# Three dense samples instead of one, and the MLP's ring tile moved into the attention

## The reference

```python
# layer 0: deformable convolution (4 groups x 9 points = 36 samples a token) and an MLP
xp = x @ w_in + b_in
h = gelu(batch_norm(depthwise_conv3x3(x)))
offset = h @ w_off + b_off
mask = softmax((h @ w_msk + b_msk).reshape(N, H, W, GROUP, P), axis=-1)
samp = corner(y0, x0, (1-wy1)*(1-wx1)) + corner(y0, x0+1, (1-wy1)*wx1) \
     + corner(y0+1, x0, wy1*(1-wx1)) + corner(y0+1, x0+1, wy1*wx1)
y = einsum('nghwpc,nhwgp->nhwgc', samp, mask) @ w_out + b_out
x = x + gamma1 * layer_norm(y)
x = x + gamma2 * layer_norm(gelu(x @ w_fc1 + b_fc1) @ w_fc2 + b_fc2)
# layer 1: causal attention over an image's 3136 tokens, then 8 experts of which 2 count
t = t + attention(layer_norm(t))
t = t + experts_top2(layer_norm(t))
```

## Time and profile before

| what | us |
|---|---|
| median of 3 runs | 8872.07 (8864.89 to 8880.12) |
| the profiled execution's own time | 8881.66 |
| its span, first to last instruction | 8879.9 |
| PE busy (weight loads beside) | 5273.8 (3409.6) |
| DVE busy | 5563.6 |
| ACT busy | 2767.3 |
| POOL busy | 6554.4 |

### The profile page before, as it was taken

How to read it: one execution, slowest core, us unless ns; L and a number is a source line. 1 busy time by engine, 2 the same in 40 slices (tenths; PEclk the granted TensorE clock), 3 DMA queues, 4 the chain that set the end, 5 groups by cost and what they waited for, 6 DMA issues and landing times.

```text
span 8879.9 us, 85702 instructions
## 1 busy us (share of the span) xinstructions
PE 5273.8 (59%) x24752; PEld 3409.6 (38%) x24752; DVE 5563.6 (63%) x12091; ACT 2767.3 (31%) x6449; POOL 6554.4 (74%) x6898
## 2 busy tenths in 40 slices
PE   4456575555755576555665567654757556564567
PEld 2234353333533354333443344432434333342345
DVE  4666666666666666666576656765666666665554
ACT  2223232323323233322333233332323233332233
POOL 6777777777777777777777777777777777777771
PEclk7778787777877788777887788876878778776778
DMA  7333333232333323333333333333233333222220
GB/s 104 72 75 69 74 70 78 66 75 69 70 77 68 76 66 73 75 72 71 68 77 70 74 68 73 75 75 68 67 79 70 73 68 65 73 65 65 62 64 15
DMA packets 851881, 625.60 MB, mean 70 GB/s; under 512 B 551018, under 2 KB 734562, under 8 KB 851472
## 3 DMA queue, kind: packets, MB, share of 16 engines
q0 software_dynamic: 221200, 452.62, 21.0%
q1 hardware_dynamic: 629600, 167.72, 11.4%
q10 hardware_dynamic: 672, 0.24, 0.0%
HBM read 549.46 MB, written 70.57 MB: 70 GB/s over the span
## 4 chain that ended last, share of the span: by engine, by line
POOL 59%; issue 22%; PE 9%; DVE 5%; DMA 4%; SPq 1%; ACT 1%; POOLq 0%; DVEq 0%; another core or an unknown queue 0%; ACTq 0%
POOL ring L707 59%; DMA ring<-column_table,idx_r 3%; PE bank L1508 2%; PE bank L1544 2%; DVE y L1042 1%; PE bank L1517 1%; PE bank L1432 1%; PE bank L1684 1%; PE bank L1596 1%; PE bank L1661 1%; SPq L523 0%; DMA wts_r<-corner_weight 0%; SPq L493 0%; DVE ring L1032 0%; DMA tokens<-z 0%
## 5 line engine op out<-in xcount | busy, mean ns | idle before, releaser
L707 POOL DMA_INDIRECT ring<-column_table,idx_r x6860 | 6530.9, 952 | 2146.0 <-issue 2069.6
L1032 DVE TENSOR_TENSOR ring<-ring,bank 128x4608 f32<-128x4608 f32 x196 | 970.1, 4949 | 1017.7 <-POOLq L718 1016.6
L1042 DVE TENSOR_REDUCE y<-ring 128x128 f32<-128x4608 f32 x196 | 1571.1, 8016 | 16.8 <-remote 14.6
L1489 PE MATMUL bank<-ident,xn 112*128 112x112 f32 x224 | 54.9, 400 | 1722.5 <-DVE xn L968 1722.5
L1508 PE MATMUL bank<-kT,qT 128*112 128x448 f32 (+3 forms) x1792 | 824.7, 552 | 159.2 <-DVE arena L1144 152.2
L1544 PEld LDWEIGHTS bank<-v,pT 112*112 112x112 f32 x6496 | 817.7, 181 | 264.2 <-issue 186.1
L1544 PE MATMUL bank<-v,pT 112*112 112x128 f32 x6496 | 851.7, 278 | 57.1 <-DVE pT L1177 57.0
L1144 DVE TENSOR_SCALAR_CACHE_REDUCE arena<-bank 112x448 f32<-112x448 f32 x672 | 416.2, 623 | 524.6 <-PE bank L1508 495.4
L1517 PE MATMUL bank<-ident,arena 112*112 112x112 f32 x3248 | 495.6, 273 | 395.4 <-ACT arena L828 395.3
L1489 PEld LDWEIGHTS bank<-ident,xn 112*128 112x128 f32 x224 | 37.1, 217 | 1731.7 <-issue 1731.7
L1432 PE MATMUL bank<-xflat,stripes 116*128 116x448 f32 (+1 forms) x1120 | 586.9, 649 | 110.7 <-ACT xflat L790 110.6
(11 more groups left out here) (179 smaller groups left out, 7291.8 us busy)
## 6 DMA issues: line engine op xcount, KB each, us to landing
ring<-column_table,idx_r POOLq DMA_INDIRECT x6860
xflat<-dense_rows SPq DMA_DIRECT2D x56, 406.0 KB
column_table<-proj SPq DMA_DIRECT2D x196, 112.0 KB
corner_weight<-wts_s SPq DMA_DIRECT2D x56, 252.0 KB
wts_r<-corner_weight SPq DMA_DIRECT2D x196, 72.0 KB
hT<-dense_rows SPq DMA_DIRECT2D x224, 56.0 KB
tin<-tokens SPq DMA_DIRECT2D x56, 224.0 KB, 3.1
out<-xn SPq DMA_DIRECT2D x56, 224.0 KB
```

Source lines behind the costliest of these rows:

```text
L707: pool.indirect_dma_start(ring[:, r, e * CORNERS:(e + 1) * CORNERS, :].rearrange("p s c -> p (s c)"), None, source, bass.IndirectOffsetOnA ...
L1032: dve.tensor_tensor(corners, corners, wts_p.unsqueeze(2).broadcast_to([128, GP * CORNERS, CG]), ALU.mult)\
L1042: dve.tensor_reduce(y[:, k % BLK % 2].rearrange("p (g c) -> p g c", g=G), ring[:, bass.ds(t % RING, 1)].rearrange("p o (g e) c -> p (o g) ...
```

## The change

It computes samples 33, 34 and 35 on PE (`DENSE = 3`) and gathers 33 (`FETCHED = GP - DENSE`). The rows stored and loaded, the places, the hats and the sums are there three times: 15 stages in a chunk (`STAGES`). Three stages (`EARLY`) stand ahead of the attention, so DVE's `set_places` moves ahead of the layer norm and xn is turned in bank 5; the other twelve stand in the row blocks, three to each. `keep_part` of the first sample stands in row block 0, of the second in row block 2, of the third in the front. The ring holds 33 samples, and `sum_up` reduces it in two instructions, of three whole groups and of the last one's six samples. `between` is gone from the MLP: h=0 now has tiles 0 (first), 1 (second), 2 (`extra`: multiplied behind q=2, reduced behind q=3) and 3 (third), h=1 has 4, 5 and 6. The memset of the ring's unused part is gone.

```diff
-FETCHED = GP - 1
+DENSE = 3
+FETCHED = GP - DENSE
+XN_BANK = 5
+EARLY = 3
+STAGES = DENSE * (NB // 2)
...
-        ring = sb("ring", [128, RING, GP * CORNERS, CG])
+        ring = sb("ring", [128, RING, FETCHED * CORNERS, CG])
...
+        rows = (xflat[0:2 * PAD], rows_b[:, :, :], rows_c)
+        place = (hT[0:2 * PAD, 1], rows_b[:, 0], rows_c[:, 0])
+        row_wts = (hT[:, 0], wts_b[:, :], wts_c[:, :])
...
-                        first, second, third, between = (
-                            ((p, n, 1), (p, n, 2), (p, n, 3), (p, n, 4)),
-                            ((p, n, 5), None, (p, n, 6), (p, n, BLK)))[h]
+                        first, second, extra, third = (
+                            ((p, n, 0), (p, n, 1), (p, n, 2), (p, n, 3)),
+                            ((p, n, 4), (p, n, 5), None, (p, n, 6)))[h]
...
-                sp.wait_ge(d_kept, FIRST + gd)
+                sp.wait_ge(d_kept, FIRST + DENSE * gd)
...
+                for k in range(DENSE):
+                    sp.dma_start(rows[k].rearrange("p a n -> p (a n)"),
+                                 row_d[gd, k, 0:2].rearrange("a n -> (a n)").partition_broadcast(2 * PAD))\
                         .then_inc(d_rows_in, 16)
+                    for dy in range(DY):
+                        sp.dma_start(row_wts[k][dy * CG:(dy + 1) * CG], row_d[gd, k, 2 + dy].partition_broadcast(CG))\
+                            .then_inc(d_rows_in, 16)
...
+                sample, pair = stage // (NB // 2), stage % (NB // 2)
+                if pair == 0:
+                    act.wait_ge(d_placed, FIRST + DENSE * gd + sample + 1)
...
+                if now:
+                    for stage in range(EARLY):
+                        hats(gd, stage)
                 act.wait_ge(xn_turned, FIRST + g + 1)
...
-                        hats(gd, q)
+                        hats(gd, EARLY + 3 * q)
...
                             exponentials(c + 2)
+                        if now and c == j // 3:
+                            hats(gd, EARLY + 3 * q + 1)
+                        if now and c == 2 * j // 3:
+                            hats(gd, EARLY + 3 * q + 2)
                     if q == 1 and second:
                         tile(*second)
-                if now:
-                    hats(gd, NT)
+                    if q == 3 and extra:
+                        tile(*extra)
...
+                step.did(dve.tensor_reduce(
+                    y[:, k % BLK % 2, 0:(G - 1) * CG].rearrange("p (g c) -> p g c", g=G - 1),
+                    products[:, 0:whole].rearrange("p (g e) c -> p g c e", g=G - 1), AX.X, ALU.add))
                 dve.tensor_reduce(
+                    y[:, k % BLK % 2, (G - 1) * CG:], products[:, whole:].rearrange("p e c -> p c e"), AX.X, ALU.add)\
                     .then_inc(y_made, 1)
...
-                if between:
-                    tile(*between)
...
+                else:
+                    dve.wait_ge(d_kept, FIRST + DENSE * gd + sample)
+                    step.did(dve.tensor_tensor(row_wts[sample], bank[0][:, 0:CH], row_wts[sample], ALU.mult))
+                    step.wait()
+                    dve.tensor_tensor(part[:, f % 2], part[:, f % 2], row_wts[sample], ALU.add).then_inc(d_kept, 1)
...
                     multiply(*first)
+                if now:
+                    set_places(dense_chunk(*now)[2])
                 dve.wait_ge(tok_in[buf], (s + h) * 16)
...
                 layer_norm(tin[:, buf], xn, NT, TT, 1e-5).then_inc(xn_made, 1)
-                if now:
-                    set_places(dense_chunk(*now)[2])
...
                             chunk_max(q + 1, c)
+                        if now and q == 0 and c == j // 3:
+                            keep_part(*now, 0)
+                        if now and q == 2 and c == 0:
+                            keep_part(*now, 1)
...
+                    if extra and q == 2:
+                        multiply(*extra)
+                    if extra and q == 3:
+                        sum_up(*extra)
...
-                        keep_part(*now)
+                        keep_part(*now, 2)
...
-                step.did(dve.memset(ring[:, :, FETCHED * CORNERS:, :], 0.0))
...
+                elif pair == 0:
+                    pe.wait_ge(d_kept, FIRST + DENSE * gd + sample)
...
                 banks_left(fronts, s * 2 + h, g)
+                if now:
+                    for stage in range(EARLY):
+                        sum_columns(di, gd, stage)
                 pe.wait_ge(xn_made, FIRST + g + 1)
...
-                        sum_columns(di, gd, q)
+                        sum_columns(di, gd, EARLY + 3 * q)
...
                         ins.then_inc(pv_made, 1)
+                        if now and c == j // 3:
+                            sum_columns(di, gd, EARLY + 3 * q + 1)
+                        if now and c == 2 * j // 3:
+                            sum_columns(di, gd, EARLY + 3 * q + 2)
...
-                if now:
-                    sum_columns(di, gd, NT)
```

More of the change, by code:

```diff
@@ L451, in slots @@
                             tile(p, n, k1 - 1)
-                        mlp(s, n, h, last, (p, fronts[h] + 1), g + 1 if att else 0, between, then)
+                        mlp(s, n, h, last, (p, fronts[h] + 1), g + 1 if att else 0, then)
             first_image()
@@ L621, in tile, with attention @@
                 ring_load(p, t)
-            def attention(i, j, h, s, fronts, first, second, now):
+            def attention(i, j, h, s, fronts, first, second, extra, now):
                 if first:
@@ L627, in attention, with mlp @@
                     tile(*second)
-            def mlp(s, n, half, last, fronts, n_att, between, then):
+                if extra:
+                    tile(*extra)
+            def mlp(s, n, half, last, fronts, n_att, then):
                 k0, k1 = PARTS[half]
@@ L793, in dense, with attention @@
             def dense(now):
[L794 removed]
+                for stage in range(STAGES):
                     hats(dense_chunk(*now)[2], stage)
[L797 removed]
+            def attention(i, j, h, s, fronts, first, second, extra, now):
                 g = i * NJ + j
                 gd = dense_chunk(*now)[2] if now else 0
+                if now:
+                    for stage in range(EARLY):
+                        hats(gd, stage)
                 act.wait_ge(xn_turned, FIRST + g + 1)
[L801 removed]
+                act.activation(xnT[:, :], bank[XN_BANK][:, 0:CH], ACT.Copy).then_inc(xnT_kept, 1)
                 act.wait_ge(qkv_made, FIRST + g * 3 + 1)
@@ L1117, in dense, with attention @@
             def dense(now):
                 set_places(dense_chunk(*now)[2])
-                keep_part(*now)
-            def attention(i, j, h, s, fronts, first, second, now):
+                for k in range(DENSE):
+                    keep_part(*now, k)
+            def attention(i, j, h, s, fronts, first, second, extra, now):
                 g = i * NJ + j
@@ L1436, in dense @@
                 i, _, gd = dense_chunk(*now)
-                for stage in range(NB // 2):
+                for stage in range(STAGES):
                     sum_columns(i, gd, stage)
-                pe.wait_ge(d_kept, FIRST + gd + 1)
+                pe.wait_ge(d_kept, FIRST + DENSE * (gd + 1))
             def project(s, k):
```

137 lines of the change are left out of this document (67 added, 70 removed).

## The result

The changed kernel takes 10,306.12 us (median of 4 runs, 10,292.80 to 10,316.14) where the kernel before takes 8,872.40: 1.1616 times as long, interval 1.1601 to 1.163. The profiled execution took 10,316.14 us, its span is 10,314.3. The experiments were run in five sets, each on one chip with the kernel before beside it. So the change costs 1,394 to 1,434 us; the forecast was 870. The other four sets ran on chips where every kernel, the one before too (14,269 to 14,353 us), takes 1.5 to 1.6 times as long, so their ratios are read against each other only.

A forecast was written before the change was run, and what follows sets the result against it. POOL's gathers bound the kernel; the chain of DVE, ACT and PE would take over. A cycle: 9 + 18 + 1 + 4 + 2 - 1 = +33 us; 7,865 + 1,782 + 100 (startup) = 9,747, so 9,750 us, range 9,100 to 10,200.

The forecast's parts named there:

- What bounds the kernel: Whole kernel: POOL's gathers at 1.254 us each are the bound; DVE waits 1,016.6 us for POOL.
- the 7,865 us of chain: DVE, ACT and PE without the waits for POOL: 8,881.7 - 1,016.6, about 134 us in each of 54 cycles.
- Early stages: Three stages ahead of xn's transposes: PE there 15.0 us after the multiply, now 4.6; +9 us a cycle, bounds 7 and 12.
- The DMAs' +2: SP's 15 row loads for five and tripled store values: late rows hold set_places; +2 us a cycle, bounds 0 and 12.
- The Trainium skill's rule on the lowest-numbered engines: Row loads: three broadcasts on the same four engines, in turn, landing at 30 us; +4 rather than +2.
- The rival of the rows' loads: Stores and three sets hold tokens and tin back, 10 us more a cycle: 10,290; rows later than 30 us; 10%.
- The q rows and the tile: Attention: two more stages a row, mean +18 us a cycle (12 to 28); ring tile moved in, mean +4 (0 to 8).
- 18 + 1 + 4: Us a cycle: stages in the q loops 18, keep_part 1, ring tile moved into the attention 4.
- The start: Two lone dense chunks: ten stages each (36 us) and two more sets of rows (13), nothing beside them; +100 us.
- The MLP and fc2: MLP without the ring tile: DVE waits 10 to 13 us for fc2 every cycle; MLP gains only 1.3 to 3.5.
- VectorE's saving: DVE's multiply and reduce shrink from 36 to 33 samples: counted as 1 us less in a cycle.
- the room on the other chain: DVE, ACT and PE chain beside POOL: even at 17 us a cycle added; all of POOL's gain kept under 9.7.

The follow-up runs named there:

- one row: Changed kernel with samples 2 and 3 taking sample 1's rows (store of 2,688 values, 5 loads): 9,897.77 us, 1.1161 times the kernel before.
- the second set: Unaltered changed kernel run again on one chip beside the kernel before: 10,258.27 us against 8,863.81, ratio 1.1568.
- the store late: Changed kernel with the dense rows' store moved behind the load of tin, three times on slower chips: 15,188 to 15,371 us, ratios 1.0664, 1.0626, 1.0705.

## Why the prediction was wrong

The direction and most of the mechanism were right. The step that failed is the term for the DMAs: it priced the loads and left out what the store does to the queue they stand in. The size was 560 us short, and the result lies beyond the range's 10,200.

- **What bounds the kernel: right.** GpSimd's waits went completely, and it now waits for the ring. The 7,865 us of chain are not tried by themselves: 7,865 + 2,407 = 10,272 for a span of 10,265.6 only shows that the bookkeeping of the two traces closes, since no run takes GpSimd's waits away and leaves the rest.
- **Early stages: right.** 15.0 us from the multiply's end, where `set_places` starts, to the transposes were forecast from the earlier trace rows. At j=3 the places begin at 6,075.00 and the transposes stand at 6,091.38, 16.4 us on, behind three stages, two of which have the long matmuls of the lower clock (3.35 us in the second, where the third has 1.77):

```profile
6084.59 3.35 PE L1473 MATMUL bank<-xflat,stripes 116*128 116x448 f32 x4 [1.83 <-ACT xflat L800]
6089.77 1.77 PE L1473 MATMUL bank<-xflat,stripes 116*128 116x448 f32 x4 [1.83 <-ACT xflat L800]
6091.38 0.55 PE L1533 MATMUL bank<-ident,xn 112*128 112x112 f32 x4
```

In the table +5.8 to the first row maximum and, with the rows' wait away, +1.8 ahead of the norm: 7.6 for the forecast 9.
- **The DMAs' +2: the step that failed.** The term named "three times the 4-byte values in store_rows" and then priced only the loads, by how long after their issue they would be there. That was about right: 22 to 28 us where VectorE waits for them, of the 10.2 to 30.5 given. But the issue itself came 9 us later, because SP stood behind the store. The term is 6.4 us a cycle, and 4.3 of it go with two thirds of the store (15.2 - 10.9). The trace of before held the hint, some 6 us ahead of the earlier trace rows: the issue behind a store of 2,688 values took 2.04 us, where the same issue takes 0.34 elsewhere. The Trainium skill's rule on the lowest-numbered engines, by which the prediction would have put 4 in its place, speaks of the loads' landing. The 22 to 28 us for three sets where one took 10.2 lie nearer to "in turn" (30.5) than to "side by side", which agrees with it but does not show it, since the 15 issues alone take 10 us of SP (4,967.89 to 4,978.09); and still its term would have been under two thirds of the measured one. The two rows of the kernel before:

```profile
4133.85 0.52 SPq L509 DMA_DIRECT2D dense_rows<-drow  x1
4134.56 2.04 SPq L603 DMA_DIRECT2D idx_r<-corner_index  x1
```

- **The rival of the rows' loads: its time was right, its condition was not.** 10,290 us stood against 10,306. But in the cycles the rows land 22 to 28 us after their issue, not later than 30, and what waits is set_places. And 234 us of the miss are not theirs, most of it the loops'. That its number came near is luck.
- **The q rows and the tile: mechanism right, size short.** +22.7 and +3.7 (the reduce behind the last row, 7.4 in the even halves against 7.5 forecast) are 26.4 us for the 23 forecast as 18 + 1 + 4. By j, from 0 to 6, the loops grew by 30, 33, 21, 19, 17, 18 and 20 us (24, 25, 19, 17, 13, 13, 13 forecast). The light ones were placed with stages of 3.6 us, at full clock; the window at j=0 has a granted clock of 0.66 (0.75 in the same loop before), and 47% of the stages' matmul records last over 0.6 us, where 0.54 is the short kind; before it was 35%. That the clock is what the light loops lack is argued from this; no run changes the clock alone.
- **The start: +100 forecast, +188 to +196 measured.** The added stages of the two lone chunks were put at 72 us and cost 93: VectorE's waits for a sample's sums are 45.6 + 45.3 + 48.6 us where one wait of 46.1 stood. The added sets of rows were put at 26 and cost 79 (one row: 467.1 for 546.0). Some 16 us of the start are in neither. Ahead of the first attention each front's store has to be out before the next dense_rows writes drow, and that wait grew from 28.9 to 79.1 us, the one for the loads from 20.9 to 71.3. VectorE's waits in the first 554 us of the changed kernel:

```profile
DVE xflat L1126 <- DMA wts_c<-dense_rows: 71.3, 3, 36.9
DVE wts_c L1144 <- PE bank L1473: 48.6, 2, 25.0
DVE part L1141 <- PE bank L1473: 45.6, 2, 25.8
DVE wts_b L1144 <- PE bank L1473: 45.3, 2, 25.7
```

- **The MLP and fc2: right.** A wait of 10 to 13 us for fc2 was forecast in every cycle, 12.0 is there, and the half gains 1.2 us.

Against the 10,258 us of the second set, 511 were missing. The cycles are 8.1 us longer than forecast (41.1 for 33), 437 us: the rows' wait 4.4, the loops and the tile 3.4, VectorE's saving, which no stretch shows, 1, front and MLP 0.6, less 1.4 at the early stages. The start is 88 us longer, 53 of it rows and 21 stages. That makes 525, of which the rows are 291 and the loops with the tile 184.

## What to carry to other kernels

Price a DMA's issue by what it does to the issues behind it in its queue, in numbers of elements and not in bytes: here 8,064 values of 4 bytes (32 KB) held SP for 11 us, while the issue behind the 72 KB of wts_r took 0.36, and what was late was the next transfer. Such a store belongs where nothing urgent is issued for as long as it takes. A serial round between two engines (hats, sums, hats) costs time on the chain even where both are often idle: three of them put 7.6 us a cycle ahead of the attention, though ACT is idle for 60% of the span and PE for 36%. In the loops eight more came with 30 us at j=0, where the granted clock was 0.66, and with 20 at j=6, where it was 1.00. When an engine that is the bound is relieved, work out the room on the other chain first (17 us a cycle here) and stop when two terms exceed it.

## What was not expected of the hardware

A store of single 4-byte values, 8,064 of them in place of 2,688, raises the time of the issue that follows it on the same queue from 2.04 and 2.28 us to 11.37 (medians 2.2 and 11.4; on the slower chips 2.2 and 10.4, and 6.0 for 5,376 values), while the store's own issue stays at 0.51 us, and an issue that comes 12.9 us or more after the store takes 0.34 (seen on the slower chips only). One instance of the same kind, behind another front, took 14.07:

```profile
4445.83 0.70 SPq L519 DMA_DIRECT2D dense_rows<-drow  x1
4446.72 14.07 SPq L616 DMA_DIRECT2D idx_r<-corner_index  x1
```

The second thing is that the same kernel can take 1.6 times as long on another chip while hardly any of it is in the instructions. VectorE's multiply of 4,949 ns takes 4,946 there. TensorE's granted clock is lower, 0.67 for 0.78, and its busy time grows from 5,274 to 5,852 us, but the span grows by 5,441. The q rows of the kernel before with its tile moved take 108.5 us where 43.8 stood, and its waits show pauses of TensorE with nothing that the profile could put them down to:

```profile
PEld bank L1553 <- issue: 1480.1, 849, 27.0
PE bank L1553 <- issue: 1261.0, 140, 26.4
```

In the kernel before on the first chip the weight loads of the same matmuls (L1544 there) have 186.1 us of "issue" in all, 0.4 at the longest. Many pauses come back at the same instruction of the same cycle in each pair of images, and they move with an edit: with the store late, 1,882 us stand in the MLP. Their cause was not found. The loads of instructions are as many and as long there (204 packets of 16 KB of 1.1 us each on queue q8, in both traces), and GpSimd's gathers go on at 945 ns each. Only a base measured on the same chip makes such a run readable, and small edits can't be judged in it.
